# The start of a fused transformer block: first four sequences in two pairs, small loads and first weights on a second queue, one vector addition less in the scales

## What is computed

```
ada = cond @ ada_w + ada_b                    # six vectors of 256 per sequence
shift1, scale1, gate1, shift2, scale2, gate2 = split(ada, 6)
x1  = ln(x) * (1 + scale1) + shift1
q, k, v = split(x1 @ qkv_w + qkv_b)           # 16 heads of width 128
a   = softmax(q k^T / sqrt(128)) v            # per sequence and head
y   = x + gate1 * (a @ out_w + out_b)
x2  = ln(y) * (1 + scale2) + shift2
z   = y + gate2 * (gelu(x2 @ ffn_w1 + ffn_b1) @ ffn_w2 + ffn_b2)
h   = relu(z @ ternary(W_fc)^T)^2
out = x + (h / rms(h)) @ ternary(W_proj)^T
```

## Time and profile before

| | |
|---|---|
| median of 3 runs | 359.79 us (358.42 to 359.95) |
| profiled execution | 358.39 us, of which span 356.6 us |
| TensorE busy | 348.0 us, 98% |
| VectorE, ScalarE, GpSimd busy | 59%, 56%, 30% |
| granted TensorE clock | 0.997 |

### The profile page before, as it was taken

One profiled execution on the slowest core, in us unless ns is written; L12 is line 12 of the kernel. 1 busy time (PEld: TensorE's weight loads), 2 busy tenths in 40 slices (PEclk: granted clock), 3 DMA queues, 4 the chain that ended last, 5 costly groups with the idle time before them and its releaser, 6 DMA issues.

```text
span 356.6 us, 5788 instructions
## 1 busy us (share of the span) xinstructions
PE 348.0 (98%) x1998; PEld 300.7 (84%) x1998; DVE 210.0 (59%) x397; ACT 201.2 (56%) x524; POOL 107.5 (30%) x97
## 2 busy tenths in 40 slices
PE   8999899999999999999999999999999999999995
PEld 7788788888888888888888888888887888788875
DVE  5762347436535743643574354557875876677796
ACT  2675454545355454546555444656479645975593
POOL 2552222322733132272313237447451100000000
PEclk9999999999999999999999999999999999999998
DMA  5962031000303100030300003001000000000002
GB/s 177 367 202 85 4 118 61 0 0 2 119 0 118 59 0 0 0 118 3 115 0 0 0 0 118 2 0 61 1 2 0 1 2 0 2 0 0 3 29 88
DMA packets 12321, 16.52 MB, mean 46 GB/s; under 512 B 704, under 2 KB 8976, under 8 KB 12304
## 3 DMA queue, kind: packets, MB, share of 16 engines
q1 hardware_dynamic: 12160, 16.17, 13.5%
q10 hardware_dynamic: 144, 0.13, 0.1%
HBM read 15.25 MB, written 1.05 MB: 46 GB/s over the span
## 4 chain that ended last, share of the span: by engine, by line
PE 72%; issue 20%; DVE 4%; ACT 1%; DMA 1%; POOL 1%; POOLq 0%; ACTq 0%; DVEq 0%
PE bank L1010 17%; PE bank L1012 16%; PE bank L1011 16%; PE bank L1058 8%; PE bank L1039 8%; PE bank L1047 4%; DMA xt<-in_x_dram 1%; PE bank L1128 1%; DVE stats L670 1%; POOL rstd L344 1%; DVE hid_lo L736 1%; PE bank L1149 0%; DVE yT L762 0%; ACT o_hi L460 0%; DVE prob L690 0%
## 5 line engine op out<-in xcount | busy, mean ns | idle before, releaser
L349 POOL TENSOR_TENSOR prob<-prob,rinv 128x512 f32<-128x512 f32 x32 | 33.3, 1042 | 148.8 <-DVE rinv L826 148.8
L495 ACT ACTIVATE prob<-bank,nbias 128x128 f32<-128x128 f32 x128 | 45.3, 366 | 40.3 <-DVE nbias L814 40.3
L811 DVE TENSOR_REDUCE negmax<-bank 128x4 f32<-128x512 f32 x32 | 22.1, 690 | 74.1 <-PE bank L1039 74.1
L1010 PE MATMUL bank<-x_hi,wqk_hi 128*128 128x512 f32 x126 | 52.5, 417 | 0.0
L1012 PE MATMUL bank<-x_hi,wqk_lo 128*128 128x512 f32 x126 | 49.6, 394 | 0.0
L1011 PE MATMUL bank<-x_lo,wqk_hi 128*128 128x512 f32 x126 | 49.2, 390 | 0.0
L460 ACT ACTIVATE o_hi<-bank,bias 128x512 fp32r<-128x512 f32 x32 | 22.0, 688 | 38.3 <-PE bank L1058 38.3
L464 ACT ACTIVATE vals<-bank 128x512 f32<-128x512 f32 x32 | 19.0, 597 | 36.5 <-PE bank L1012 35.6
L1058 PEld LDWEIGHTS bank<-probT,vals 128*128 128x128 f32 x256 | 33.5, 191 | 2.5
L744 DVE TENSOR_SCALAR kT<-bank,bias 128x512 f32<-128x512 f32 x32 | 24.0, 751 | 19.2 <-PE bank L1012 19.1
L1039 PE MATMUL bank<-kT,qT 128*128 128x128 f32 x256 | 33.9, 275 | 1.0 <-DVE ada L852 1.0
(11 more groups left out here) (174 smaller groups left out, 768.8 us busy)
## 6 DMA issues: line engine op xcount, KB each, us to landing
raw_qk<-in_L_cond_qkv_w_dram SPq DMA_DIRECT2D x6, 512.0 KB, 4.5
raw_v<-in_L_cond_qkv_w_dram SPq DMA_DIRECT2D x4, 512.0 KB, 4.1
raw_o<-in_L_cond_out_w_dram SPq DMA_DIRECT2D x4, 512.0 KB, 3.5
xt<-in_x_dram SPq DMA_DIRECT2D x2, 512.0 KB, 4.4
xr<-in_L_cond_ada_w_dram SPq DMA_DIRECT2D x1, 1024.0 KB, 8.6
raw_w<-in_L_cond_ffn_w_dram SPq DMA_DIRECT2D x2, 512.0 KB, 6.8
t_raw<-in_L_ffn_W_fc_dram SPq DMA_DIRECT2D x4, 256.0 KB, 3.7
t_raw<-in_L_ffn_W_proj_dram SPq DMA_DIRECT2D x4, 256.0 KB, 3.9
```

Of the source, the lines that this page charges most:

```text
L349: nc.gpsimd.tensor_tensor(e, e, rinv[:, j % 2, :].unsqueeze(2).broadcast_to([P, SQ, P]), ALU.mult).then_inc(norm_done, 1)
L495: e = nc.scalar.activation(prob[:, j % 2, s, :], bank[BS][:, s * P:(s + 1) * P], ACT.Exp, bias=nbias[:, j % 2, s:s + 1], scale=SCALE, accu ...
L811: nc.vector.tensor_reduce(negmax[:, j % 2, :], bank[BS][:, :].rearrange("p (s t) -> p s t", s=SQ), axis=AX.X, op=ALU.max, negate=True).the ...
L1010: nc.tensor.matmul(dst, ah, bh, start=start and n == 0, stop=False)
```

## The change

Loads: x of the first quad is loaded as two pairs with a semaphore each. The condition, ada_b and head 0's query and key weights are issued from ScalarE's queue, ahead of ScalarE's other work. SyncE no longer waits for x; value weights and x of the second quad are issued ahead of the biases.

Normalisation: for the first quad the statistics, the power and the normalising are done pair by pair (`stats_half`, `rstd_half`, `normalise_half`).

Low part of head 0's weights: VectorE makes it, between the two pairs, instead of GpSimd.

Scales: 1.0 is added once to the bias columns of both scales (`scale_bias`), and `ada_part` is a single instruction in both places.

TensorE: 9 and 9 throwaway transposes in place of 14 and 12.

```diff
--- before.py
+++ after.py
@@ -158,14 +158,16 @@
 
         cond_in, arow_in, bias_in, ada1_in, ada2_in = (
             sem(n) for n in ("cond_in", "arow_in", "bias_in", "ada1_in", "ada2_in"))
-        x_in = [sem(f"x{n}_in") for n in range(NQ)]
+        x0_in, x1_in = [sem("x0a_in"), sem("x0b_in")], sem("x1_in")
+        st0_done, mv0_done, ve0_done, rstd0_done = (sem(n) for n in ("st0_done", "mv0_done", "ve0_done", "rstd0_done"))
+        scale_bias = sem("scale_bias")
         wqk0_in = sem("wqk0_in")
         wqk_in, wv_in, wo_in, tern_in = sem("wqk_in"), sem("wv_in"), sem("wo_in"), sem("tern_in")
         w1_in, w2_in, out_done_dma = sem("w1_in"), sem("w2_in"), sem("out_stored")
 
         zeroed, ident_set, half_set = sem("zeroed"), sem("ident_set"), sem("half_set")
         small_t, small_cp = sem("small_t"), sem("small_cp")
-        ada_mm, ada_ready, ada_sum = sem("ada_mm"), sem("ada_ready"), sem("ada_sum")
+        ada_mm, ada_ready = sem("ada_mm"), sem("ada_ready")
         st_done, mv_done, ve_done, rstd_done, xn_done, xt_done = (
             sem(n) for n in ("st_done", "mv_done", "ve_done", "rstd_done", "xn_done", "xt_done"))
         mod_a, mod_d, xs_hi, xs_lo = sem("mod_a"), sem("mod_d"), sem("xs_hi"), sem("xs_lo")
@@ -253,17 +255,14 @@
 
         @block.sync
         def _(sp):
-            sp.dma_start(xt[:, 0:SQ, :], x[0:SQ].rearrange("b t d -> t b d")).then_inc(x_in[0], 16)
-            sp.dma_start(crow, cond).then_inc(cond_in, 16)
-            sp.dma_start(arow, ada_b.rearrange("(n p) -> n p", p=P)).then_inc(arow_in, 16)
+            for h in range(2):
+                s = slice(h * SQ // 2, (h + 1) * SQ // 2)
+                sp.dma_start(xt[:, s, :], x[s].rearrange("b t d -> t b d")).then_inc(x0_in[h], 16)
             sp.dma_start(ada_w1, ada_w[:, 0:2 * D].rearrange("(k p) n -> p k n", p=P)).then_inc(ada1_in, 16)
-            sp.wait_ge(x_in[0], 16)
-            for s in range(2):
-                sp.dma_start(raw_qk[:, s * KD:(s + 1) * KD, 0:P], qkv_v[0, s][:, :, 0:P]).then_inc(wqk0_in, 16)
+            sp.dma_start(raw_v[:, :, :], qkv_v[0, 2]).then_inc(wv_in, 16)
+            sp.dma_start(xt[:, SQ:B, :], x[SQ:B].rearrange("b t d -> t b d")).then_inc(x1_in, 16)
             for src, at, n in ((qkv_b, QB, 3 * H), (out_b, OB, KD), (ffn_b1, F1B, NC), (ffn_b2, F2B, KD)):
                 sp.dma_start(brow[at - NA:at - NA + n, :], src.rearrange("(n p) -> n p", p=P)).then_inc(bias_in, 16)
-            sp.dma_start(raw_v[:, :, :], qkv_v[0, 2]).then_inc(wv_in, 16)
-            sp.dma_start(xt[:, SQ:B, :], x[SQ:B].rearrange("b t d -> t b d")).then_inc(x_in[1], 16)
             for s in range(2):
                 sp.dma_start(raw_qk[:, s * KD:(s + 1) * KD, P:HG * P], qkv_v[0, s][:, :, P:HG * P]).then_inc(wqk_in, 16)
             sp.dma_start(ada_w2, ada_w[:, 2 * D:6 * D].rearrange("(k p) n -> p k n", p=P)).then_inc(ada2_in, 16)
@@ -336,12 +335,19 @@
             def rstd_of(e):
 
                 s = slice(e * SQ, (e + 1) * SQ)
-                pool.wait_ge(mv_done, e + 1)
+                pool.wait_ge(mv_done, e)
                 nc.gpsimd.tensor_scalar(var_eps[:, s], mv[:, s, 1], LN_EPS, 1.0, ALU.add, ALU.mult).then_inc(ve_done, 1)
-                if e == 0:
+                pool.wait_ge(ve_done, e)
+                nc.gpsimd.tensor_tensor(rstd[:, s], var_eps[:, s], neg_half[:, :], ALU.pow).then_inc(rstd_done, 1)
+
+            def rstd_half(h):
+                s = slice(h * SQ // 2, (h + 1) * SQ // 2)
+                pool.wait_ge(mv0_done, h + 1)
+                nc.gpsimd.tensor_scalar(var_eps[:, s], mv[:, s, 1], LN_EPS, 1.0, ALU.add, ALU.mult).then_inc(ve0_done, 1)
+                if h == 0:
                     pool.wait_ge(half_set, 1)
-                pool.wait_ge(ve_done, e + 1)
-                nc.gpsimd.tensor_tensor(rstd[:, s], var_eps[:, s], neg_half[:, :], ALU.pow).then_inc(rstd_done, 1)
+                pool.wait_ge(ve0_done, h + 1)
+                nc.gpsimd.tensor_tensor(rstd[:, s], var_eps[:, s], neg_half[:, 0:SQ // 2], ALU.pow).then_inc(rstd0_done, 1)
 
             def normalise(i, j):
                 pool.wait_ge(rinv_done, i + 1)
@@ -388,9 +394,8 @@
                 if j == 6:
                     wqk_lo_part(2, HG * G + HG + 3)
 
-            rstd_of(0)
-            pool.wait_ge(xn_done, 1)
-            wqk_lo_part(0, 1)
+            rstd_half(0)
+            rstd_half(1)
             pool.wait_ge(xs_lo, KD)
             for k in range(KD):
                 wv_lo_part(k, k + 1)
@@ -536,6 +541,10 @@
                 if vs:
                     keep_v(vs[1], v_count(G, j, 1), BQ)
 
+            act.dma_start(crow, cond).then_inc(cond_in, 16)
+            act.dma_start(arow, ada_b.rearrange("(n p) -> n p", p=P)).then_inc(arow_in, 16)
+            for s in range(2):
+                act.dma_start(raw_qk[:, s * KD:(s + 1) * KD, 0:P], qkv_v[0, s][:, :, 0:P]).then_inc(wqk0_in, 16)
             act.wait_ge(small_t, 1)
             nc.scalar.activation(condT[:, :, :], bank[7][:, 0:KD * B].rearrange("p (k b) -> p k b", k=KD), ACT.Copy).then_inc(small_cp, 1)
             act.wait_ge(small_t, 2)
@@ -669,29 +678,45 @@
                 for s in range(SQ):
                     m = nc.vector.bn_stats(stats[:, e * SQ + s, :], src[:, quad * SQ + s, :])
                 m.then_inc(st_done, 1)
-                dve.wait_ge(st_done, e + 1)
+                dve.wait_ge(st_done, e)
                 for s in range(SQ):
                     m = nc.vector.bn_aggr(mv[:, e * SQ + s, :], stats[:, e * SQ + s, :])
                 m.then_inc(mv_done, 1)
 
             def normalise(e, src):
                 quad = e % NQ
-                dve.wait_ge(mv_done, e + 1)
-                dve.wait_ge(rstd_done, e + 1)
+                dve.wait_ge(mv_done, e)
+                dve.wait_ge(rstd_done, e)
                 if e == 1:
                     dve.wait_ge(xt0_done, SQ // 2)
                 if e > 1:
                     dve.wait_ge(xt_done, e - 1)
                 if e == NQ:
                     dve.wait_ge(w1_l, 4)
-                xn_e = xn2 if e >= NQ else xn1 if e else xn
+                xn_e = xn2 if e >= NQ else xn1
                 for s in range(SQ):
                     n = e * SQ + s
                     m = nc.vector.tensor_scalar(xn_e[:, s, :], src[:, quad * SQ + s, :], mv[:, n, 0:1], rstd[:, n:n + 1],
                                                 ALU.subtract, ALU.mult)
-                    if e == 0 and s < SQ - 1:
-                        m.then_inc(xn0_done, 1)
                 m.then_inc(xn_done, 1)
+
+            def stats_half(h):
+                s0 = h * SQ // 2
+                dve.wait_ge(x0_in[h], 16)
+                for s in range(s0, s0 + SQ // 2):
+                    m = nc.vector.bn_stats(stats[:, s, :], xt[:, s, :])
+                m.then_inc(st0_done, 1)
+                dve.wait_ge(st0_done, h + 1)
+                for s in range(s0, s0 + SQ // 2):
+                    m = nc.vector.bn_aggr(mv[:, s, :], stats[:, s, :])
+                m.then_inc(mv0_done, 1)
+
+            def normalise_half(h):
+                dve.wait_ge(mv0_done, h + 1)
+                dve.wait_ge(rstd0_done, h + 1)
+                for s in range(h * SQ // 2, (h + 1) * SQ // 2):
+                    nc.vector.tensor_scalar(xn[:, s, :], xt[:, s, :], mv[:, s, 0:1], rstd[:, s:s + 1],
+                                            ALU.subtract, ALU.mult).then_inc(xn0_done if s < SQ - 1 else xn_done, 1)
 
             def modulate(e, shift, scale, src, between=None):
 
@@ -839,28 +864,32 @@
                 if j in ((3, 4) if last else (4, 7)):
                     ternary_compare(G, -1 if j == (4 if last else 7) else 1)
 
-            dve.wait_ge(x_in[0], 16)
-            stats_of(0, xt)
-            normalise(0, xt)
-
-            def ada_part(n, c0, c1, s0, src):
-                dve.wait_ge(small_cp, 2)
+            stats_half(0)
+            stats_half(1)
+            normalise_half(0)
+            dve.wait_ge(wqk_h, 1)
+            nc.vector.tensor_tensor(wqk_lo[:, :, 0:P], raw_qk[:, :, 0:P], wqk_hi[:, :, 0:P].bitcast(F32), ALU.subtract).then_inc(wqk_l, 1)
+            dve.wait_ge(small_cp, 2)
+            scales = bias[:, SCALE1:SCALE1 + NA].rearrange("p (a c) -> p a c", a=2)[:, :, 0:KD]
+            nc.vector.tensor_scalar(scales, scales, 1.0, None, ALU.add).then_inc(scale_bias, 1)
+            normalise_half(1)
+
+            def ada_part(n, c0, c1, src):
+                dve.wait_ge(scale_bias, 1)
                 dve.wait_ge(ada_mm, 1 + SQ * n)
                 nc.vector.tensor_tensor(ada[:, c0:c1, :], src[:, c0 * B:c1 * B].rearrange("p (c b) -> p c b", b=B),
-                                        bias[:, c0:c1].unsqueeze(2).broadcast_to([P, c1 - c0, B]), ALU.add).then_inc(ada_sum, 1)
-                dve.wait_ge(ada_sum, n + 1)
-                nc.vector.tensor_scalar(ada[:, s0:s0 + KD, :], ada[:, s0:s0 + KD, :], 1.0, None, ALU.add).then_inc(ada_ready, 1)
-
```

(12 more changed lines are left out.)

## The result

The changed kernel takes 363.62 us (median of 6, 361.7 to 364.19) against 359.87 us for the kernel before on the same chip (median of 6, 358.38 to 360.08): ratio 1.0103, 95% interval 1.007 to 1.0137. Its profiled execution took 364.19 us, span 362.4.

What follows compares the result with a forecast made beforehand. TensorE, busy 98% of the span, bounds the kernel; only its start and one wait count. 1.6 + 0.2 less 0.1 gives 1.7 us: 356.7 from the profiled execution, 358.1 from the median; forecast 358.0, range 356.4 to 359.5.

Steps and rivals of the forecast that it cites:

- Frame: TensorE runs almost without a gap from 12.38 us, so an earlier start moves everything behind it by the same time.
- Part 1, the step that failed: Loads at the start: first scale weights issued at about 1.65 us, landing at 6.15, bounds 5.6 and 7.0.
- I put this at nothing: SyncE without its wait on x, later loads issued sooner: no effect on their first users, bounds -0.2 to +0.3.
- rival B: Scale weights land late, at 7.0 us; modulation at 9.3, gain only 1.3 us, 358.5 us; chance 0.10.
- Part 1, head 0's weights: Head 0's query and key weights take 2.9 us to land, about 5.0, before VectorE needs them at 6.7.
- Part 2: Normalising by pairs: first pair lands 3.50 us, power done 5.92, normalising from 6.04; all complete at 8.5 against 8.99.
- Part 3: Scales at the start: product ends at 8.2, the 1.12 us operation goes, modulation at 8.8 instead of 10.40: 1.6 us gained.
- Part 4: Second table, TensorE's 1.0 us wait before the long loop: one VectorE operation gone, 0.2 us gained, lower bound zero.
- A (port): Normalising on VectorE is blocked by GpSimd's second power until 7.39; gain only 0.6 us, 359.2 us; chance 0.17.
- C (slower): Pauses from fewer transposes keep TensorE slow at the start: product 3.7 us, loss of 1.1 us, 360.9 us; chance 0.10.

Runs made afterwards that it cites:

- last kernel but one: Changed kernel, head 0's weights on SyncE's queue behind its x wait, low part on GpSimd, 12 and 12 transposes, TensorE's table wait inside the loop: 356.59 us, ratio 0.9922.
- single addition alone: Kernel before with only the scales part: 1.0 added once to the bias, each table update one operation; 358.61 us, ratio 0.9987.
- the wait was moved: Kernel before with TensorE's wait for the table of scales moved from ahead of the long loop to the first out product inside it: 357.29 us, ratio 0.9932.

## Why the prediction was wrong, step by step

- **Frame** (a start moved by some time moves everything): held at the start. 3.9 us at 12 us are 4.1 at 38. But it was not complete: a pause of TensorE has a price beyond its length, and not every lead survives. The whole gain "from 12.38 on" was taken as kept; of the 1.1 us of the single addition the profiled execution kept 0.6 and the fastest 1.0, and a start 0.6 earlier (10.84 against 11.44) kept nothing. The base, too, mixed two groups of executions 1.6 us apart.
- **Part 1, the step that failed**: "they are issued at about 1.65 and land at 6.15", bounds 5.6 and 7.0. They were issued at 1.73 and landed at 8.3. With the wait kept, head 0's weights behind it and only the small loads on the second queue (last kernel but one) they land at 6.2, so the estimate was right for loads that stay behind. The bulk behind them on the same queue, issued at 3.3 instead of 5.1, makes it 6.9; head 0's weights on the second queue with the bulk held back, 7.7; both, 8.3. "I put this at nothing" was said of exactly the edit that cost this. The trace of before had said so by omission: the 385 GB/s of the earlier trace rows were measured with one queue in use, and every load I moved forward would have to share them. What the Trainium skill ("DMA: Bandwidth & Descriptors", section "Issuing engines are not separate DMA queues") says against the change, that the two queues share the engines, agrees with these traces: 7.7 instead of 6.2 for the scale weights, and x at 5.1 instead of 4.2. I gave it only the size of rival B.
- **Part 1, head 0's weights**: "about 5.0", bounds only through the scale weights; they landed at 10.3. The 2.9 us of the earlier trace rows was read from a moment (issue at 4.20) when only the scale weights were still ahead and the value weights were issued 2.4 us later. As VectorE has their low part between the pairs, they, not the power, set the second pair.
- **Part 2**: right to about 0.15 us as far as it ran undisturbed: first pair landed 3.5, power done 5.8 (0.72 us for two numbers a row, below the 1.04 taken), normalising from 5.88.
- **Part 3**: the operation of 1.12 us did sit behind GpSimd, and without it 1.1 us are gained at the start (single addition alone). "TensorE ... to 6.1, just where the scale weights land" left no reserve: the 9 throwaway transposes end at 6.7 (at 6.3 where ada_b lands in time), the weights came 1.6 later.
- **Part 4**: 0.2 gained was forecast, 0.2 lost was measured. The removed operation is gone, but VectorE's update starts 0.5 us after TensorE's last product instead of 0.1.
- **Rivals**: A (port) is refuted: normalising at 5.88 runs beside the power at 6.13, both near their usual length (0.73 and 0.72 us). The exclusive lock of the Trainium skill ("SBUF — State Buffer", section "SBUF: two separate sides") is not seen for the power here. C (slower) had the mechanism, half pace after a pause, with its product of 3.7 us (3.55 measured), and half of the cause: the fewer transposes cost time because they end before a late load (with 14 and 18 of them the product took 1.92 us). It got a chance of 0.10 only, and its first sentence misread: the clock record has no entry at 2.5 us, its first one in before is the rise at 6.38 us, and the slow transposes ahead of it ran at the lower of the two levels. B had the late load at half its size. Each was priced as if the other did not happen; together they are the result.

What stays open: whether 9 and 9 transposes would cost anything with the loads as before; whether the short pause alone or also the eight-column product behind it puts the rise of the clock off to 14 us and later; why VectorE's update before the loop starts 0.4 us late in every kernel made from the changed one, except where the wait was moved and it no longer matters; and which of the later waits takes back a lead of more than about 1 us.

## What to carry to other kernels

A wait of the issuing engine can be a throttle that keeps bulk transfers away from the one that is needed next: before it is removed or a load put on another queue, add up what is then in flight at the same time, and price the load on the critical path by that, not by its old duration. Where TensorE waits for a load behind warm-up work, size that work by the latest landing, and price a pause at its length plus what follows at half pace. Read TensorE's pace at the start from the spacing of like matmuls, since a window ahead of the clock record's first entry says 1.00. And look at single execution times: two groups a fixed amount apart were a mechanism here that could be removed.

## What the runs showed of the hardware

- 256 KB issued on a second queue at 0.73 us delayed a 512 KB load issued at the same moment on the first by 0.9 us (4.4 instead of 3.45 us); the same 256 KB on the first queue behind the scale weights, issued at 2.51 us, delayed neither of the two 512 KB loads ahead of them by more than 0.1.
- TensorE starts at half pace (identity transposes 213 ns apart) and the rise to full clock (110 ns) came at 4.25 to 7.08 us in eleven profiled executions, while TensorE did little but throwaway transposes. In three executions TensorE stopped before the rise, for 0.83, 1.60 and 1.79 us from 6.2 to 6.7 us on, and the rise came at 13.9, 17.1 and 15.7 us. Pauses of 0.30, 0.59 and 0.79 us after the rise left the pace full; one of 1.04 us after it was followed by a fall to 0.50 at 8.84 us. The windows read 1.00 ahead of the first entry of the clock record.
- Eight-column matmuls with a pause of 0.7 to 1.2 us behind them make the granted clock fall to 0.50 for about 3.4 us in a part of the executions, at a cost of 1.6 us. Of 20 executions of before in one series 11 took 358.3 to 358.5 us with a mean clock of 0.996 or more, and 8 took 359.8 to 360.2 with 0.993 or less (one took 361.3). With the wait moved, four executions lie within 0.12 us.
- GpSimd's power takes 0.72 us for two numbers a row and 1.01 to 1.04 for four.
